# The last stage of a four-stage image kernel: loads taken from SBUF, one tile prepared earlier, stores issued by another engine

## The reference

```python
patches = _unfold(x, oh, ow)                 # 3x3 windows at stride 2: (B, C, 3, 3, 128, 128)
x1 = patches.max(axis=1).reshape(B, K * K, oh, ow)        # maxima over the channels
x2 = patches.max(axis=2).reshape(B, C * K, oh, ow)
x3 = patches.max(axis=3).reshape(B, C * K, oh, ow)
feat = jnp.concatenate([x1, x2, x3], axis=1)              # 9 + 96 + 96 features
y = jnp.einsum('bihw,oi->bohw', feat, conv_w)             # 1152 outputs of each pixel
y = jax.nn.relu((y - bn_mean[...]) * inv + bn_beta[...])
w = y.reshape(B, C, K * K, NEW, NEW, oh, ow)
out = jnp.mean(patches.reshape(B, C, K * K, 1, 1, oh, ow) * w, axis=2)
x = x + out                                                # 2x2 outputs of each window
```

## Time and profile before

| | before |
|---|---|
| median of 3 runs | 3263.21 us |
| the profiled execution's own time | 3277.86 us |
| its span (first to last instruction) | 3276.0 us |
| PE, DVE busy | 2748.8 us (84%), 2654.4 us (81%) |
| POOL, ACT busy | 1831.2 us (56%), 1817.2 us (55%) |
| TensorE's mean granted clock | 0.930 of full speed |

### The profile page before, as it was taken

One profiled execution on the slowest core, in us unless ns is written; L12 is line 12 of the kernel. 1 busy time (PEld: TensorE's weight loads), 2 busy tenths in 40 slices (PEclk: granted clock), 3 DMA queues, 4 the chain that ended last, 5 costly groups with the idle time before them and its releaser, 6 DMA issues. The chain is left out here.

```text
span 3276.0 us, 45677 instructions
## 1 busy us (share of the span) xinstructions
PE 2748.8 (84%) x12765; PEld 2135.7 (65%) x12765; DVE 2654.4 (81%) x3575; ACT 1817.2 (55%) x2351; POOL 1831.2 (56%) x1296
## 2 busy tenths in 40 slices
PE   0087698899989779799989769889998977979998
PEld 0036586777747658577765658677775765857776
DVE  8986987788884888688888598778888489868887
ACT  7753655656552655566655265566655265556654
POOL 2013272799940446299990327279994044629998
PEclk9998899999997889899999689999999788989999
DMA  6732002899840200789880200289985020078984
GB/s 252 251 102 71 1 0 69 228 223 227 188 155 3 68 0 0 189 217 228 208 212 35 71 1 0 69 226 224 226 188 155 2 69 0 0 189 216 229 209 113
DMA packets 116199, 419.22 MB, mean 128 GB/s; under 512 B 16565, under 2 KB 30693, under 8 KB 105354
## 3 DMA queue, kind: packets, MB, share of 16 engines
q1 hardware_dynamic: 96058, 374.65, 44.5%
q10 hardware_dynamic: 18432, 38.54, 3.3%
q0 software_dynamic: 1616, 4.90, 0.5%
HBM read 340.57 MB, written 75.26 MB: 127 GB/s over the span
## 5 line engine op out<-in xcount | busy, mean ns | idle before, releaser
L920 POOL TENSOR_TENSOR work<-work 128x512 f32<-128x512 f32 x960 | 1283.3, 1342 | 411.0 <-DVE work L1340 310.4
L575 PE MATMUL psum<-workr,w 128*128 128x512 f32 (+1 forms) x5760 | 1366.0, 397 | 67.2 <-ACT workr L792 50.6
L575 PEld LDWEIGHTS psum<-workr,w 128*128 128x128 f32 (+1 forms) x5760 | 1085.9, 189 | 346.6 <-issue 51.4
L1331 DVE SCALAR_TENSOR_TENSOR work<-psum,work 128x512 f32<-128x512 f32 x1152 | 738.2, 679 | 34.0 <-POOL work L920 21.4
L544 PE MATMUL psum<-workr 128*128 128x512 f32 x2304 | 550.9, 401 | 21.5 <-DVE workr L1228 21.5
L894 POOL TENSOR_TENSOR work<-img 128x520 f32 (+1 forms) x256 | 387.7, 1545 | 283.7 <-DVE workr L1200 254.3
L544 PEld LDWEIGHTS psum<-workr 128*128 128x128 f32 x2304 | 439.7, 191 | 134.2 <-issue 24.7
L884 POOL TENSOR_TENSOR work<-work 128x1024 f32<-128x1024 f32 x40 | 112.9, 2856 | 479.1 <-DVE work L1113 479.1
L772 ACT CAST workr<-psum 128x650 fp32r<-128x650 f32 x128 | 90.0, 703 | 419.2 <-DVE psum L1307 419.2
L440 PE MATMUL psum<-work,taps 128*128 x1152 | 261.6, 391 | 44.4 <-DVE work L1064 44.4
L1304 DVE TENSOR_TENSOR psum<-psum,work 128x650 f32<-128x650 f32 x128 | 107.9, 843 | 208.4 <-ACT psum L765 208.2
(11 more groups left out here) (188 smaller groups left out, 3506.1 us busy)
## 6 DMA issues: line engine op xcount, KB each, us to landing
work<-gn_dram SPq DMA_DIRECT2D x256, 585.0 KB, 10.6
work<-gn_dram SPq DMA_DIRECT2D x256, 146.2 KB, 3.9
work<-gn_dram SPq DMA_DIRECT2D x128, 292.5 KB, 4.8
work<-in_x SPq DMA_DIRECT2D x16, 2048.0 KB, 7.3
img<-in_x SPq DMA_DIRECT2D x32, 1024.0 KB, 11.4
work<-in_mixw SPq DMA_DIRECT2D x64, 512.0 KB, 5.3
out_x<-work ACTq DMA_DIRECT2D x120, 256.0 KB, 6.2
gn_dram<-img SPq DMA_DIRECT2D x24, 1040.0 KB, 16.6
```

Source lines behind the costliest of these rows:

```text
L575: mm = T.matmul(bank(m % 6), w5[wt][0:kr, P * n:P * n + P], ft[0:kr], start=(i == 0), stop=(i == 4))
L920: G.tensor_tensor(acc_t[v], acc_t[v], pd_t[(9 * v + n) % 6], ALU.add).then_inc(s_acc, 1)
L1331: V.scalar_tensor_tensor(out=tile4(pd_t[m % 6]), in0=tile4(psum[:, m % 6, :]), scalar=0.0, in1=rv[:, q, y0:y0 + RT, x0:x0 + WO], op0=ALU.m ...
```

## The change

Four things are changed, all in the last stage.

1. `gn_dram`, `store_rows` and their semaphores are gone. `load_planes` and `load_pixels` read from `img` in SBUF. Since an SBUF access takes its partitions from one range, a pair's pixels are now 16 DMAs of 32 partitions by 1170 elements where they were four of 32 by 4 by 1170. Behind the last pair SP waits until all planes and pixels have landed, ahead of the next image's rows, which go into `img`.
2. The first tile's features (`front(0, 0, 0, ...)` on DVE, `prepare(0)` on ACT) are made while the maxima are taken: DVE's three steps stand behind the reductions 20, 21 and 24 (`FIRST`), ACT's copies ahead of the maxima's. The transposed maxima use PSUM bank 5, not 0, so PE can fill banks 0 to 4 ahead of them.
3. The two restores of the first pair stand behind both tiles' features on ACT.
4. The stores of finished tiles are issued by SP: `store(2 * i)` ahead of the maxima and pixels of pair i+1, and `store(2 * i + 1)` behind them. The last two tiles' stores stay on POOL.

```diff
+FIRST = (20, 21, 24)
...
-        mxq = psum[:, 0, :].rearrange("p (m2 m1 w) -> p m1 m2 w", m2=2, m1=2)
+        mxq = psum[:, 5, :].rearrange("p (m2 m1 w) -> p m1 m2 w", m2=2, m1=2)
...
                 def load_planes(u8, k):
...
-                    sp.dma_start(a_t[k][0:32, :], gn_dram[0:32, n9]).then_inc(s_ab3[k], 16)
+                    sp.dma_start(a_t[k][0:32, :], img[0:32, n9]).then_inc(s_ab3[k], 16)
...
                 def load_pixels(u8, k):
-                    for n in range(4):
-                        sp.dma_start(r_t[k][32 * n:32 * n + 32, :].rearrange("p (q n) -> p q n", q=4),
-                                     byq[:, :, ds(u8 * PW, 9 * PW)]).then_inc(s_inr[k], 16)
-
-                def store_rows(e):
-
-                    hold(sp, s_gn3, b * NCH + (e + 1))
-                    r0 = 0 if e == 0 else 1 + CR * e
-                    r1 = HO + 2 if e == NCH - 1 else 1 + CR * (e + 1)
-                    sp.dma_start(gn_dram[:, r0 * PW:r1 * PW], img[:, r0 * PW:r1 * PW]).then_inc(s_gnd[e], 16)
+                    for q in range(4):
+                        for n in range(4):
+                            sp.dma_start(r_t[k][32 * n:32 * n + 32, 9 * PW * q:9 * PW * (q + 1)],
+                                         img[32 * q:32 * q + 32, ds(u8 * PW, 9 * PW)]).then_inc(s_inr[k], 16)
+
+                def store(n):
+
+                    hold(sp, s_acc, b * NADDS + (n // 2 * ADDS + pool_adds(n % 2, 8) + 8))
+                    sp.dma_start(out[b, :, TILE * n:TILE * n + TILE], acc_t[n % 4]).then_inc(s_out[n % 4], 16)
 
                 def load_next(i):
 
                     p = i % 2
                     if i < NPAIR - 2:
                         if i % 2 == 0:
-                            hold(sp, s_gnd[i // 2 + 1], b * 16 + 16)
+                            hold(sp, s_gn3, b * NCH + (i // 2 + 2))
                         hold(sp, s_fmax, b * NT + (2 * i + 2))
                         load_planes(RP * (i + 2), p)
+                    store(2 * i)
                     hold(sp, s_pd, b * (9 * NT) + (18 * i + 18))
                     load_maxima(sp, RP * (i + 1), (p + 1) % 2)
                     load_pixels(RP * (i + 1), (p + 1) % 2)
+                    store(2 * i + 1)
...
                 for i in range(NPAIR - 1):
                     load_next(i)
-                    if i % 2 == 1 and i // 2 + 3 < NCH:
-                        store_rows(i // 2 + 3)
+                for p in range(2):
+                    hold(sp, s_ab3[p], b * (96 * (NPAIR // 2)) + 96 * (NPAIR // 2))
+                    hold(sp, s_inr[p], b * (256 * (NPAIR // 2)) + 256 * (NPAIR // 2))
...
                 for n in range(6):
+                    if n == 5:
+                        pe.wait_ge(s_mxz, b * 4 + 4)
+                        pe.wait_ge(s_mxl, b * 2 + 2)
                     product(n, n, terms, range(4))
...
+                def prepare(k):
+
+                    shifted(0, 0, k)
+                    high(0, 0, k, free=False)
+                    side_high(0, 0, k)
+                    side_low(0, 0, k)
+
+                act.wait_ge(s_tail, b * 32 + 16)
+                act.wait_ge(s_guard, b * 3 + 3)
+                prepare(0)
                 act.wait_ge(s_mxp, b * (NT + 1) + (NT + 1))
...
-                def store(j, v):
-                    act.wait_ge(s_acc, b * NADDS + j * (2 * ADDS) + (v // 2 * ADDS + pool_adds(v % 2, 8) + 8))
-                    act.dma_start(out[b, :, ds(j * (4 * TILE) + v * TILE, TILE)], acc_t[v % 4]).then_inc(s_out[v % 4], 16)
...
+                prepare(1)
                 for k in range(2):
-                    shifted(0, 0, k)
-                    high(0, 0, k, free=False)
-                    side_high(0, 0, k)
                     restore(0, k)
-                    side_low(0, 0, k)
...
-                    store(j, 2 * p)
...
-                    store(j, 2 * p + 1)
...
+                for n in range(NT):
+                    v.wait_ge(s_mxp, b * (NT + 1) + (n + 1))
+                    V.tensor_reduce(mx_rq[:, RT * n:RT * n + RT, :],
+                                    psum[:, 2 + n % 4, :].rearrange("p (r q c) -> p r q c", r=RT, q=4), AX.X, ALU.max
+                                    ).then_inc(s_mxr, 1)
+                    if n in FIRST:
+                        front(0, 0, 0, FIRST.index(n))
...
-                for k in range(2):
-                    for step in range(3):
-                        front(0, 0, k, step)
+                for step in range(3):
+                    front(0, 0, 1, step)
```

More of the change, by code:

```diff
@@ L109, in build @@
         SMALL_BANK = 6
-        gn_dram = nc.dram_tensor("gn_dram", (P, IMG_N), F32, kind="Internal").ap()
         bn_dram = nc.dram_tensor("bn_dram", (2, 9 * P), F32, kind="Internal").ap()
@@ L250, in build @@
         s_gn3 = sem("s_gn3")
-        s_gnd = [sem(f"s_gnd{e}") for e in range(NCH)]
         s_mxp, s_mxr, s_mxz, s_mxd = sem("s_mxp"), sem("s_mxr"), sem("s_mxz"), sem("s_mxd")
@@ new lines, in load_planes @@
+                    sp.dma_start(b_t[k][0:32, PW:10 * PW], img[32:64, n9]).then_inc(s_ab3[k], 16)
+                    sp.dma_start(a_t[k][64:128, :], img[0:64, n9]).then_inc(s_ab3[k], 16)
+                    sp.dma_start(a_t[k][32:64, :], img[64:96, n9]).then_inc(s_ab3[k], 16)
+                    sp.dma_start(b_t[k][32:64, PW:10 * PW], img[96:128, n9]).then_inc(s_ab3[k], 16)
+                    sp.dma_start(b_t[k][64:128, PW:10 * PW], img[64:128, n9]).then_inc(s_ab3[k], 16)
+                def load_pixels(u8, k):
+                    for q in range(4):
+                        for n in range(4):
+                            sp.dma_start(r_t[k][32 * n:32 * n + 32, 9 * PW * q:9 * PW * (q + 1)],
+                                         img[32 * q:32 * q + 32, ds(u8 * PW, 9 * PW)]).then_inc(s_inr[k], 16)
@@ L747, in _ @@
                                  ).then_inc(s_gn3, 1)
-                act.wait_ge(s_mxp, b * (NT + 1) + (NT + 1))
-                for v in (0, 2):
-                    A.copy(mzq[:, v, :, 1:3, :], mxq).then_inc(s_mxz, 1)
-                    A.copy(mzq[:, v, :, 0, 1:WO], mxq[:, :, 1, 0:WO - 1]).then_inc(s_mxz, 1)
-                act.wait_ge(s_mxz, b * 4 + 4)
-                act.wait_ge(s_mxl, b * 2 + 2)
-                act.wait_ge(s_guard, b * 3 + 3)
-                act.dma_start(mx_dram[0:HO, MXI:MXR], mz.bitcast(F32)).then_inc(s_mxd, 16)
-                act.dma_start(mx_dram[1:HO + 1, 0:MXI], mz[:, MXI:2 * MXI].bitcast(F32)).then_inc(s_mxd, 16)
                 def shifted(j, p, k):
@@ L809, in _ @@
                     side_high(0, 0, k)
+                    side_low(0, 0, k)
+                act.wait_ge(s_tail, b * 32 + 16)
+                act.wait_ge(s_guard, b * 3 + 3)
+                prepare(0)
+                act.wait_ge(s_mxp, b * (NT + 1) + (NT + 1))
+                for v in (0, 2):
+                    A.copy(mzq[:, v, :, 1:3, :], mxq).then_inc(s_mxz, 1)
+                    A.copy(mzq[:, v, :, 0, 1:WO], mxq[:, :, 1, 0:WO - 1]).then_inc(s_mxz, 1)
+                act.wait_ge(s_mxz, b * 4 + 4)
+                act.wait_ge(s_mxl, b * 2 + 2)
+                act.wait_ge(s_guard, b * 3 + 3)
+                act.dma_start(mx_dram[0:HO, MXI:MXR], mz.bitcast(F32)).then_inc(s_mxd, 16)
+                act.dma_start(mx_dram[1:HO + 1, 0:MXI], mz[:, MXI:2 * MXI].bitcast(F32)).then_inc(s_mxd, 16)
+                prepare(1)
+                for k in range(2):
                     restore(0, k)
-                    side_low(0, 0, k)
                 def step(j, p, more=True):
@@ L1291, in _ @@
                 mx_rq = mxt.rearrange("p (q r) -> p r q", q=4)
-                with v.Fori(0, NT // 4) as j:
-                    for k in range(4):
-                        v.wait_ge(s_mxp, b * (NT + 1) + j * 4 + (k + 1))
-                        V.tensor_reduce(mx_rq[:, ds(j * (4 * RT) + k * RT, RT), :],
-                                        psum[:, 2 + k, :].rearrange("p (r q c) -> p r q c", r=RT, q=4), AX.X, ALU.max
-                                        ).then_inc(s_mxr, 1)
                 def front(j, p, k, step):
```

17 lines of the change are left out of this document (3 added, 14 removed).

## The result

| | before | changed |
|---|---|---|
| median | 3270.91 us (3260.43 to 3278.74, 4 runs) | 3699.24 us (3689.22 to 3710.36, 4 runs) |
| ratio | | 1.130, 95% interval 1.125 to 1.135 |
| profiled execution, own time | 3277.86 us | 3710.36 us |
| its span | 3276.0 us | 3708.5 us |

The change makes the kernel 13% slower. Forecast were 3609 us and a range of 3440 to 3740: the direction and the place are right, the size is 90 us short. (The forecast was set against the median of three runs of before; a fourth run moved that median from 3263.21 to 3270.91.)

What follows compares the result with a forecast made beforehand. PE, POOL and the DMA engines stood close together as bounds. Per image +92.2 - 3.6 - 2.2 = +86.4 us, for four +345.6, giving 3609 us against the median; range 3440 to 3740.

Steps and rivals of the forecast that it cites:

- The wait for POOL's tile ahead of the pixels: On SP, each pair: the even tile's store waits for POOL until 14.6 us after the pair's start, holding back the pixels.
- From the store to the last landing: Each pair: store, maxima and pixels take 13.0 us, making the period 27.6 instead of 21.5 us, +92.2 us an image.
- The issue: On SP: one pixel DMA issue takes 0.44 us, so a pair's sixteen take 7.0 us.
- rival 1: Pixel loads: narrow loads run faster from SBUF and issue sets the pace; period 25.0 us, 3453 us in all; chance 0.13.
- Start: Each image's last-stage start: faster mx_dram write gains 7.3 us, early features cost 3.5; -3.6 us taken.
- End: End of each image's last stage: POOL has caught up during the wait, about -2.2 us.
- PE's clock, at no cost: PE in each pair: its clock falls in a pause, costing at most 1.7 us where six are spare: nothing.
- Signs named beforehand: Changed kernel's profile, last-stage pairs: what DVE's wait, POOL's idling, pixel issues, pair spacing and transfer rate should show.
- Against the whole: Whole kernel: last-stage terms sum to +86.4 us an image, +345.6 us for four, giving 3609 us.

Runs made afterwards that it cites:

- e1_act_stores: Changed kernel with the stores of finished tiles issued by ACT again, the rest kept: 3213.95 us, 0.986 against before.
- e2b_later_stores: Changed kernel with SP's stores moved behind the next pair's pixels, the odd tile's one pair later: 3194.71 us, 0.977 against before.
- e4_sp_stores_dram: Kernel before, with gn_dram and four pixel DMAs kept, only the stores moved to SP in the changed kernel's places: 3738.36 us, one run.
- e9_hold_landed: Changed kernel with SP waiting until a pair's pixels have landed before issuing the odd tile's store and next planes: 3651.52 us, one run.
- e5_half_bytes: Changed kernel with each of sixteen pixel pieces cut to 585 of 1170 numbers from an image's third pair on: 3574.89 us, one run.
- e8_sources_only: Kernel before with planes and pixels read from img in SBUF, nothing else of the change: 3279.13 us, 1.003 against before.
- e3_early_only: Kernel before with only the first tile's features made among the reductions, maxima in bank 5, restores behind both tiles' features: 3228.07 us, one run.
- e6_8x64: Changed kernel with a pair's pixels in eight DMAs of 64 partitions instead of sixteen of 32: 3698.83 us, one run.
- e7_4x128: Changed kernel with a pair's pixels in four DMAs of 128 partitions instead of sixteen of 32: 3365.61 us, one run.
- e2_pixels_first: Changed kernel with SP's even-tile store moved behind the next pair's pixels, both stores there: 3273.48 us, 1.001 against before.

## Why the prediction was right, and where its sizes were not

- **The wait for POOL's tile ahead of the pixels.** Right, and shown from both sides (e1_act_stores and e2b_later_stores without it, e4_sp_stores_dram with it alone). POOL's tile at T + 14.6 was measured as T + 14.67, in the pair shown and in the mean of all; taking the backlog-free 11.4 us of the first pair for it was sound.
- **From the store to the last landing: the step that was mis-sized.** Forecast 13.0 us, with maxima and pixels at 220 GB/s; measured 15.0 in the pair shown and 14.9 in the mean, so a period of 29.6 instead of 27.6 us and +122.3 instead of +92.2 us for 15 pairs. That is 30 us an image, 120 in all, more than the whole miss. e9_hold_landed splits the 1.9 us of the mean: 0.75 us because the odd tile's store and the planes, which by the prediction "come behind the pixels", are issued behind them but flow beside the last of them; 0.8 us because the same 2.77 MB take 12.8 us and not 12.0; and 0.3 us because the time around the flow is 1.3 us in two parts and not 1.0 in one. Why the flow is slower than forecast, with the DMA engines busy 91% of it in the window shown, stays open; the issue pace of 0.6 to 0.7 us a piece is near.
- **The issue.** Forecast 0.44 us from the pieces out of DRAM; from SBUF one takes 0.59 us at the median, 10 us or more for sixteen. So rival 1, with its 7.0 us of issues and a period of 25.0, had no room: e5_half_bytes, with half the bytes, still needs 10.0 us of issues and a period of 27.4.
- **Start.** Forecast -3.6, measured -5.5, and its split was wrong. The write to `mx_dram` did speed up (SP's load issued 1459.50 - 1453.78 = 5.7 us after the first write, as forecast), and the reductions did get longer: they end 3.0 us later, against 3.5 forecast. But the prediction let the early features give nothing back. e8_sources_only shows that without them the faster write is worth nothing. Two chains ended nearly together; each part hid the other's worth. With the features ready PE does its first 24 matmuls (1450.75 to 1456.59) while the maxima are on their way.
- **End.** Forecast -2.2, measured -1.3.
- **PE's clock, at no cost.** Right: 0.65 just behind the pause, and DVE's wait at each later pair's start is for pixels.
- **Signs named beforehand.** DVE's wait about 6 us (9.4 in the pair shown, 10.3 in the mean), POOL idle 7 us a pair (8.35), pixels issued from T + 15.5 (T + 15.48), 16 issues in 7 us (10.7), period 27 to 28 (29.6), rate near 220 (211 in the window, 225 over the 14.3 us).
- **Against the whole.** +463.7 us in the last stages, not +345.6; and -32.0 us in the other stages, which no step of the prediction had. The two misses partly cancel. Without the second the same sum would give some 3727 us on the 3263 us that the forecast started from: still in the range, near its end. So the mechanism was no luck, but part of the closeness to 3609 was.

## What to carry to other kernels

A queue that loads is in order: before a store is moved to it, ask when its wait ends and which loads stand behind it, then put it where its wait is already over (here one pair later), and both the loads and the freed engine gain. When two edits act on chains that end together, price them together: each alone reads as nothing. A wait that moves a load costs the load's whole way: silence ahead of its first byte and behind its last, and a share for whatever is issued before it has landed.

## What the runs showed of the hardware that I had not expected

**Steps of 16 us in a stage that nobody touched.** From an image's handoff to the next S the time is either about 392.4 us or 375 to 377 us. Before: 392.2, 392.4, 392.4. Changed: 375.3, 392.5, 377.2. e1_act_stores, e2b_later_stores, e3_early_only: 375 to 377 three times each. e8_sources_only: 375.2, 392.6, 392.4. The runs' times of one kernel lie 16 us apart for the same reason (before: 3243, 3260, 3278 us). The runs' mean granted clocks go with it: about 0.94 at 3243 us, 0.935 at 3261, 0.929 at 3278. It is PE's granted clock in the Fourier stage. Windows of the changed kernel in a short image, then at the same distance from the handoff in a long one:

```profile
1128.60:1138.60 10.00, 9.02 (x83) 8.81 (x82) 8.14 (x13) 5.37 (x10) 0.00 (x0) 1.00 0.01 2
1138.60:1148.60 10.00, 10.00 (x92) 10.00 (x91) 2.83 (x13) 0.96 (x3) 0.00 (x0) 1.00 0.00 0
```
```profile
2005.20:2015.20 10.00, 9.02 (x84) 8.81 (x81) 8.15 (x13) 5.77 (x10) 0.00 (x0) 1.00 0.01 2
2015.20:2025.20 10.00, 10.00 (x55) 10.00 (x54) 2.34 (x14) 0.79 (x2) 0.00 (x0) 0.56 0.00 0
2025.20:2035.20 10.00, 10.00 (x48) 10.00 (x49) 0.69 (x1) 0.59 (x1) 0.00 (x0) 0.50 0.01 2
```

The same matmuls, 92 in 10 us against 48, run at 1.00 (2.4 GHz) in the one and for some 30 us near 0.50 (1.2 GHz) in the other, although PE was busy 9.02 of the 10 us ahead in both and all the time behind. In the traces of before, changed, e1_act_stores, e2b_later_stores and e8_sources_only all six long passes have this stretch, some 90 us behind the handoff, and none of the nine short ones has. What decides between them stays open. It bears on every comparison here. The span of e2b_later_stores is 82.8 us shorter than before's: 34 of these are its last stages, 48 the three steps in the other stages. Of e1_act_stores' 64.7 us some 19 are its last stages'. What the change is worth with the stores put right is the smaller figure, about 1%. That the short way came in all three images of both traces, in all four runs of e2b_later_stores and in three of the four of e1_act_stores (the fourth took 3231 us), was seen but not explained; e6_8x64, e7_4x128 and e9_hold_landed have it three times too, e2_pixels_first and e5_half_bytes twice of three, e4_sp_stores_dram once.

**Issue by source.** A DMA of 32 partitions by 1170 took SP 0.31 us (L357) or 0.42 us (L358) out of DRAM before, at the median of 64 each, and 0.59 us (L364, 1024 of them, none under 0.51) out of SBUF.
